# Two accumulators of a mixture of experts: added onto a tile in SBUF by GpSimd's DMA, in place of loads and sums

## The reference, cut to what matters

```python
x = L0_attn_q                                # (2, 1024, 256)
xn = _layernorm(x)
s = _L0_attn_ref(xn, ...)
g = _silu(_L0_ffn_ref(xn, ...))              # sum of 8 chosen experts + shared expert
x = x + s * g
xn = _layernorm(x)
s = _L1_attn_ref(xn, ...)
g = _silu(_L1_ffn_ref(xn, ...))
x = x + s * g
```

```python
moe_out = _moe_experts(x, topk_idx, topk_w, w_gate, w_up, w_down)
out = moe_out + _shared_mlp(x, sh_gate, sh_up, sh_down)
```

## Time and profile before

| what | us |
|---|---|
| median of 3 runs (lowest, highest) | 421.01 (420.65, 421.41) |
| profiled execution | 421.63 |
| its span, first to last instruction | 419.9 |

### The profile page before, as it was taken

The page is one execution under the profiler, slowest core; times in us unless marked ns, Lnnn a source line. Parts: engine busy times, 40 slices in busy tenths (PEclk is TensorE's granted clock), DMA queues, the critical chain, the costliest instruction groups (busy, mean ns, idle before and its releaser), DMA issues.

```text
span 419.9 us, 6972 instructions
## 1 busy us (share of the span) xinstructions
PE 339.9 (81%) x2044; PEld 256.6 (61%) x2044; DVE 312.6 (74%) x989; ACT 213.9 (51%) x540; POOL 234.6 (56%) x219
## 2 busy tenths in 40 slices
PE   0999649998976788989989898884078888988893
PEld 0984425665754656767867667652057767877772
DVE  4599744667899496849786886834669988899875
ACT  3754424334545244476446444411156788777781
POOL 3610072767767368777777787845166655663311
PEclk9999957999999799999999999987559999999999
DMA  8956941776767298988787787535910000000001
GB/s 262 382 183 201 352 139 39 166 151 136 175 152 180 66 258 187 253 220 221 171 190 172 166 187 154 91 46 84 311 54 2 25 2 26 27 27 25 9 21 51
DMA packets 34041, 58.41 MB, mean 139 GB/s; under 512 B 3835, under 2 KB 20563, under 8 KB 33875
## 3 DMA queue, kind: packets, MB, share of 16 engines
q1 hardware_dynamic: 21715, 39.08, 29.6%
q0 software_dynamic: 12288, 18.88, 24.4%
HBM read 40.22 MB, written 17.73 MB: 138 GB/s over the span
## 4 chain that ended last, share of the span: by engine, by line
PE 34%; DVE 22%; issue 17%; POOL 10%; ACT 8%; DMA 8%; POOLq 0%; DVEq 0%; ACTq 0%
DMA acc_d<-W,idxE 5%; POOL acc_d L498 4%; PE two L1451 4%; PE two L1714 4%; PE two L1590 3%; PE two L1403 3%; POOL W L479 2%; PE two L1556 2%; PE two L1461 2%; DVE W L1111 2%; DVE A L996 2%; PE two L1477 2%; POOL ny L544 2%; PE two L1413 2%; PE two L1681 2%
## 5 line engine op out<-in xcount | busy, mean ns | idle before, releaser
L498 POOL DMA_INDIRECT acc_d<-W,idxE x64 | 101.7, 1590 | 52.3 <-DVE W L1111 28.1
L479 POOL DMA_INDIRECT W<-tok_d,idxE x56 | 56.8, 1015 | 46.5 <-DVE idxE L1067 29.8
L710 ACT ACTIVATE W<-two 128x256 f32<-128x256 f32 x64 | 24.4, 381 | 75.4 <-PE two L1579 70.8
L1154 DVE SCALAR_TENSOR_TENSOR W<-W,two 128x88 f32<-128x88 f32 x64 | 15.4, 241 | 47.0 <-ACT W L726 42.2
L1714 PE MATMUL two<-W,A 128*128 128x257 f16 x256 | 30.0, 273 | 10.7 <-DVE F L1333 9.9
L686 ACT ACTIVATE A<-two 128x512 f16<-128x512 f32 x32 | 19.1, 597 | 31.7 <-PE two L1535 22.8
L1714 PEld LDWEIGHTS two<-W,A 128*128 128x128 f16 x256 | 24.0, 98 | 16.3 <-DVE F L1333 11.7
L1681 PE MATMUL two<-F,wfcT 128*128 128x256 f16 x256 | 32.5, 281 | 1.5 <-DVE F L1271 1.4
L797 ACT ACTIVATE two<-two,gwv 128x512 f32<-128x512 f32 x32 | 21.4, 668 | 23.9 <-PE two L1681 23.9
L1590 PE MATMUL two<-W 128*128 128x176 f32 x160 | 32.0, 324 | 0.0
L1556 PE MATMUL two<-A,v_hi 128*128 128x256 f16 x128 | 24.5, 296 | 9.1 <-DVE A L996 9.0
(11 more groups left out here) (240 smaller groups left out, 900.2 us busy)
## 6 DMA issues: line engine op xcount, KB each, us to landing
W<-in_gu SPq DMA_DIRECT2D x20, 352.0 KB
acc_d<-F SPq DMA_DIRECT2D x2, 2176.0 KB, 14.4
F<-in_gu SPq DMA_DIRECT2D x12, 352.0 KB
W<-in_dn SPq DMA_DIRECT2D x20, 176.0 KB
tok_d<-xr SPq DMA_DIRECT2D x2, 1280.0 KB, 5.9
F<-in_dn SPq DMA_DIRECT2D x12, 176.0 KB
x<-in_q SPq DMA_DIRECT2D x4, 512.0 KB, 6.7
A<-in_Wo SPq DMA_DIRECT2D x1, 2048.0 KB, 12.4
```

What stands on the lines that cost most here:

```text
L479: pool.indirect_dma_start(out=xg[n % XR], out_offset=None, in_=tok_d[:, :], in_offset=bass.IndirectOffsetOnAxis(ap=idxE[:, n:n + 1], axis=0))\
L498: pool.indirect_dma_start(out=acc_d[n % 2][:, :], out_offset=bass.IndirectOffsetOnAxis(ap=idxE[:, n:n + 1], axis=0), in_=ysb[n % YS], in_o ...
L710: sc.activation(xgT[n % 2], bk_(2)[:, 0:D].rearrange("p (k n) -> p k n", k=KH), ACT.Copy)\
```

## The change

The tile `tot` becomes `xn` itself, which holds the weighed rows of the shared expert. GpSimd issues, for each pair and each accumulator, one plain DMA with an addition (`accum_op`), from the accumulator in HBM onto the pair's rows in SBUF (`add_acc`). Pairs 0 and 1 come straight after the last scatter, pairs 2 and 3 in step -3, ahead of the first root, and the pairs 4 to 7 one in each of the steps -1 to 2, between `add_gated` and `finish`. The first accumulator's DMA waits for the weighed rows; the second's waits on GpSimd until the first has landed on the same rows (`acc_ld[p]` at 16). SP's loads, VectorE's `first_total`, and GpSimd's `total` and `add_shared` are gone; the gate, `first_gated` and `gated` wait for both DMAs (`acc_ld[p]` at 32). VectorE's `shared_weighed` counts a semaphore and no longer waits for its own last instruction.

```diff
-        acc1 = F[:, 10752:14848].rearrange("p (t d) -> p t d", t=NT)
...
-        tot = W[:, 0:4096].rearrange("p (t d) -> p t d", t=NT)
+        tot = xn
...
-            def load_acc(i, p):
-
-                sp.dma_start(pair((tot, acc1)[i], p), acc_v[i][:, 0:NT, :].rearrange("p (s i) d -> p s i d", s=2)[:, :, p, :])\
-                    .then_inc(acc_ld[p], 16)
-
-            sp.wait_ge(y_ps, NE)
-            sp.wait_ge(y_added[0], 16 * (NE // 2))
-            load_acc(0, 0)
-            load_acc(0, 1)
-            sp.wait_ge(y_added[1], 16 * (NE // 2))
-            load_acc(1, 0)
-            load_acc(1, 1)
-            for p in range(2, NP):
-                load_acc(0, p)
-                load_acc(1, p)
...
-            def total(p):
+            def add_acc(i, p):
+
+                if p == 0:
+                    pool.wait_ge(y_added[i], 16 * (NE // 2))
+                if i == 0:
+                    pool.wait_ge(weighed, NT // 4)
+                else:
+                    pool.wait_ge(acc_ld[p], 16)
+                pool.dma_start(pair(tot, p), acc_v[i][:, 0:NT, :].rearrange("p (s i) d -> p s i d", s=2)[:, :, p, :],
+                               accum_op=ALU.add).then_inc(acc_ld[p], 16)
+
+            def gated(p):
+
+                pool.wait_ge(s0_ready, NT)
                 pool.wait_ge(acc_ld[p], 32)
-                then(pool.tensor_tensor(pair(tot, p), pair(tot, p), pair(acc1, p), ALU.add))
-
-            def add_shared(p):
-
-                pool.tensor_tensor(pair(tot, p), pair(tot, p), pair(xn, p), ALU.add).then_inc(acc_ready, 1)
...
+            for i in range(2):
+                for p in range(2):
+                    add_acc(i, p)
             for p in range(-AHEAD, NP):
                 if p >= 0:
                     weigh(p)
                 if 1 < p + AHEAD < NP:
-                    if p < 0:
-                        total(p + AHEAD)
-                        add_shared(p + AHEAD)
                     gated(p + AHEAD)
-                if 0 <= p and p + 1 + AHEAD < NP:
-                    total(p + 1 + AHEAD)
                 if p >= -2:
                     roots(p)
-                if p == -1:
-                    total(p + 1 + AHEAD)
-                if -1 <= p and p + 1 + AHEAD < NP:
-                    pool.wait_ge(own_ready, p + 2)
-                    add_shared(p + 1 + AHEAD)
+                if p == -AHEAD:
+                    for i in range(2):
+                        add_acc(i, 2)
+                        add_acc(i, 3)
                 if 0 < p + AHEAD < NP:
                     add_gated(p + AHEAD)
+                if -1 <= p and p + 2 + AHEAD < NP:
+                    add_acc(0, p + 2 + AHEAD)
+                    add_acc(1, p + 2 + AHEAD)
                 if 0 <= p < LAST:
                     finish(p)
...
             def gate(p):
-                if p >= 2:
-                    sc.wait_ge(acc_ready, p - 1)
-                else:
-                    sc.wait_ge(tot_first, p + 1)
+                sc.wait_ge(acc_ld[p], 32)
...
                 for t in range(t0, t1):
-                    last = mark(ve.tensor_scalar(xn[:, t, :], xn[:, t, :], den[:, t:t + 1], None, ALU.mult))
-                ve.wait_ge(dve, last)
+                    ins = ve.tensor_scalar(xn[:, t, :], xn[:, t, :], den[:, t:t + 1], None, ALU.mult)
+                ins.then_inc(weighed, 1)
...
-            first_total(0)
             first_gated(0)
...
-                if p == -2:
-                    first_total(1)
```

More of the change, by code:

```diff
@@ L275, in build @@
         sc_ready, sig_ready = sem("sc_ready"), sem("sig_ready")
-        tot_first, silu_first, x1_first = sem("tot_first"), sem("silu_first"), sem("x1_first")
+        weighed, silu_first, x1_first = sem("weighed"), sem("silu_first"), sem("x1_first")
         xT_ps, xT_ready, logits_ps, tanh_ready, bks_ready = [sem(n) for n in (
@@ L292, in build @@
             "sc_ps", "nmax_ready", "probs_ready", "pT_ps", "pT_hi_ready", "pT_lo_ready", "o_ps", "oT_ready", "wo_ps", "s0_ready")]
-        acc_ready, gated_ready, gate_ready, silu_ready, x1_ready, xh_ready, xT1_ps, xT_hi_ready, xT_lo_ready = [
-            sem(n) for n in ("acc_ready", "gated_ready", "gate_ready", "silu_ready", "x1_ready", "xh_ready", "xT1_ps",
+        gated_ready, gate_ready, silu_ready, x1_ready, xh_ready, xT1_ps, xT_hi_ready, xT_lo_ready = [
+            sem(n) for n in ("gated_ready", "gate_ready", "silu_ready", "x1_ready", "xh_ready", "xT1_ps",
                              "xT_hi_ready", "xT_lo_ready")]
@@ L501, in _ @@
                     .then_inc(y_added[n % 2], 16)
-            def total(p):
-                pool.wait_ge(acc_ld[p], 32)
-                then(pool.tensor_tensor(pair(tot, p), pair(tot, p), pair(acc1, p), ALU.add))
-            def add_shared(p):
-                pool.tensor_tensor(pair(tot, p), pair(tot, p), pair(xn, p), ALU.add).then_inc(acc_ready, 1)
+            def add_acc(i, p):
[7 more added lines that the diff above has]
+                               accum_op=ALU.add).then_inc(acc_ld[p], 16)
             def gated(p):
                 pool.wait_ge(s0_ready, NT)
-                pool.wait_ge(acc_ready, p - 1)
+                pool.wait_ge(acc_ld[p], 32)
                 pool.tensor_tensor(pair(s0, p), pair(s0, p), pair(tot, p), ALU.mult).then_inc(gated_ready, 1)
@@ L1207, in newton, with first_gated @@
                 then(ve.scalar_tensor_tensor(out=y, in0=t_, scalar=1.5, in1=y, op0=ALU.add, op1=ALU.mult))
-            def first_total(p):
+            def first_gated(p):
                 ve.wait_ge(acc_ld[p], 32)
[L1212 to L1217, removed]
                 then(ve.tensor_tensor(pair(s0, p), pair(s0, p), pair(tot, p), ALU.mult))
```

## The result

The changed kernel takes 440.1 us (median of 4; 437.42 to 440.62) against 420.86 (4 runs): ratio 1.044, interval 1.040 to 1.048. It is 19 us slower; the sum of the prediction had 27.5 more.

What follows compares the result with a forecast made beforehand. No engine is full, so the order of waits counts, stage by stage. 421.6 + 6.6 (first root at the seam) + 3.4 (pair 0) + 14.7 (three other pairs) + 2.8 (clock) = 449 us; range 432 to 468.

Steps and rivals of the forecast that it cites:

- four stops of TensorE: Layer 2, before weigh of pairs 0 to 3: TensorE stands over 5 us per pair, then no more.
- not slower: Rival, chance 0.06: issue costs GpSimd 0.05 us, data lands 1.8 us from the issue; 421.1 us, no change.
- dear: Rival, chance 0.27: issue grows with the runs to 2.7 to 3.1 us, landing 2.7 to 3.7; 462 to 473 us.
- forecast's own case: Whole kernel: issue about 1.6 us, time 443 to 455 us; chance 0.45.
- the cheap one: Rival, chance 0.22: issue 1.0 us as the gather, landing 2.25 as the scatter; 435 us, clock unchanged.
- issue g: GpSimd's time to issue one adding DMA: 1.6 us, the scatter's own price; bounds 0.99 and 3.1.
- landing L: Time from the end of an adding DMA's issue to its landing: 2.7 us; bounds 1.8 and 3.7.
- restart after a landing: On GpSimd, after a wait for a landing, 0.69 us pass until the next issue starts.
- sum of a pair's delay: Layer 2, pairs 0 to 3: two DMAs after add_gated take 7.0 us; spreads 3.4 us later once, 4.9 three times.
- The seam: Between the layers: DMAs of pairs 0 to 3 on GpSimd hold the first root until 308.9, 6.6 us late.
- The clock: After each TensorE stop the granted clock falls near 0.5; turn and square sums cost 0.7 us more, four times: 2.8.
- gain at the second root: Without GpSimd's total and add_shared, VectorE's products start 1.2 us sooner; add_gated(2) ends at 318.45, not 319.61.

Runs made afterwards that it cites:

- experiments 1 and 4: Changed kernel with the two DMAs of each of pairs 4 to 7 in GpSimd's gaps: 424.36 us; changed kernel without the second accumulator's DMAs: 415.7 us.
- experiment 2: Changed kernel with the second DMAs of pairs 2 and 3 behind the first root, not ahead of it: 437.24 us, ratio 1.040 to the kernel before.
- experiment 3: Changed kernel with pairs 4 to 7's DMAs in GpSimd's gaps and pairs 2 and 3's second DMAs behind the first root: 421.67 us, ratio 1.0037.
- experiment 8: The mixed version with VectorE's last sum for pair 1 put behind the first root: 419.95 us, ratio 0.998 to the kernel before.
- mixed version: The kernel of experiment 3, but SP loads pairs 0 and 1 and VectorE adds them onto the weighed rows: 419.26 us, ratio 0.998.
- experiment 6: The mixed version: experiment 3's kernel with pairs 0 and 1 loaded by SP and summed by VectorE: 419.26 us, ratio 0.998 to the kernel before.
- experiment 5: Changed kernel with plain DMAs in place of adding ones, same places and waits: 428.89 us, ratio 1.019 to the kernel before.

## Why the prediction was right

The direction, the place and the mechanism were right. GpSimd's queue holds finish and weigh behind the second DMA of a pair (experiments 1 and 4), and the root behind those of pairs 2 and 3 (experiment 2); with both waits out of the way 0.5 us of the tail's 19.3, or 1.6 us by the ratio, is left (experiment 3). The four stops of TensorE came where they were forecast, and no more after them. The "not slower" case fails on its price: the landing takes 4.6 us, not 1.8. The "dear" case fails too: the issue does not grow to 2.7 us with the runs.

The time, 440.1, lies in the range of 432 to 468, but below the 443 to 455 of the forecast's own case and above the 435 of the cheap one: the issue came out near the cheap case's, the landing beyond the forecast's. That these two partly cancel was luck. The terms of the sum were all too high; their sizes:

- **The issue g** was put at 1.6 and is 1.21. "Cheap" had 1.0. The scatter was too dear a neighbour: 256 runs without indices cost less than its 128 with them. That the indices make the difference is not tested.
- **The landing L** was put at 2.7 after the issue and is 3.4 (4.6 - 1.2), near its upper bound of 3.7, so the "cheap" case misses here; for the first DMA of most pairs it is 3.2 (4.4 - 1.2). The restart after a landing was put at 0.69, the scatter's, and is 0.29 (294.56 to 294.85). From the start of the first DMA to that of the second 5.0 us were forecast and 4.66 measured (335.99 to 340.65).
- **The sum of a pair's delay** was 7.0 us between add_gated and finish. It measures 5.8 (7.68 - 1.27 - 0.62): 0.3 from the items above on the way to the second DMA, 0.4 from its own issue, and the rest because there is no gap of 0.30 ahead of the first DMA and finish follows closely. That makes 4.0 us a pair in place of 4.9.
- **The seam** was 6.6 and is 4.9. Up to the second DMA of pair 2 the sizes cancel, cheaper issues and restarts against landings of up to 6.4 us: it starts 16.1 us after the last scatter (301.57 - 285.45), 16.4 were forecast. The gain lies behind it: the last two issues and the root took 3.8 us up to `newton`, not 5.2, and 0.5 of that is the root, which takes 1.09 us without VectorE's sum for pair 1 beside it (experiment 8). The prediction had put that sum at nothing.
- **The clock** was put at 2.8, 0.7 for each of four stops, and cost some 0.2 each in the profiled execution. The granted clock stood at 1.00 in the stop itself and fell only after TensorE began again (0.59 over 3.2 us), when turn and square sums were well under way: they took 1.00 us against 0.82 before. That it fell so late was luck, the price was right: in experiment 2, at 0.50 from the turn's start, the same instructions took 1.52 us, the 0.7 more that were forecast. The profiled execution is the fastest of the changed kernel's, at the highest mean clock (0.934; the others 0.92 to 0.928), so what the clock costs the others is open. The slow projections behind them used up the 1.6 us that TensorE had idle in a pair; its next wait for VectorE (L1714 before, L1689 after) is gone.
- **The gain at the second root** was there, as forecast. VectorE's products, released by ScalarE's key and value rows, start 10.7 us after the first `newton` (305.35 to 316.05), not 11.9 (303.90 to 315.77): 1.2 us. `newton` of pair 1 starts 0.8 us sooner, and before, its first instruction took 1.23 us beside GpSimd's total, where 0.16 is usual. Timelines of VectorE, before and after:

```profile
313.19 1.23 DVE L1205 TENSOR_TENSOR nt<-ny 128x4 f32<-128x4 f32 x1 [0.76 <-POOL ny L544]
```

```profile
316.05 0.35 DVE L1259 SCALAR_TENSOR_TENSOR F<-two,kvscale,F 128x128 f32<-128x128 f32 x1 [0.66 <-ACT F L774]
```

The prediction set a rule aside for the scatter's row: the Trainium skill (DMA: Bandwidth & Descriptors, "Anatomy of one DMA") fits one DMA issued on GpSimd as 2.0 us plus its bytes at 436 GB/s, an estimate of 2.6 us for 256 KB. The plain DMA here took 3.2 us and the adding one 4.6, so the traces differ from it, most where the DMA adds.

Left open: what sets the length of layer 1 in a single execution, when in or after a stop the clock falls, and whether the mixed version beats the kernel before.

## What to carry to other kernels

A DMA that must wait for another's landing holds everything behind it on the engine that issues it; put it where that engine waits for something else anyway, and price the wait by what stands behind it, not by the work that the DMA saves. To price an operation that the trace lacks, take neighbours on both sides, and keep issue and landing apart: here one was cheaper and the other dearer than the nearest row. Where an early part of the program varies by a per cent, compare tails from a common instruction.

## What the runs showed of the hardware

- An adding DMA of 256 KB from HBM into SBUF: 1.21 us of issue on GpSimd and 4.6 us from issue to landing; a plain one 0.74 and 3.2.
- With several adding DMAs in flight at the seam the landing rose to 6.4 us; alone, in the pairs, it is 4.3 to 4.8.
- The next instruction on GpSimd starts about 0.8 us after a DMA's start (327.94 to 328.73), ahead of the issue's end in the trace, and itself reads 0.5 us longer (finish 1.75 against 1.27). Its end shows that the issue holds it all the same.
- GpSimd's root takes 1.54 us beside VectorE's sum of two SBUF tiles and 1.04 without it (experiments 6 and 8).
- The other way round, a VectorE instruction of 0.16 to 0.17 us lasted 1.23 us beside GpSimd's total (313.19 to 314.42, kernel before) and 2.92 us beside finish, weigh and gated (experiment 5), each time to GpSimd's end within 0.03 us.
- The granted clock fell inside a stop of TensorE of 3 to 4 us (0.85, experiment 2), after one (0.59 over the 3.2 us behind it, changed kernel), or not at all (1.00 through a stop of 3.4 us and the turn behind it, experiment 2).
